# Where two activation buffers lie in SBUF: yT_hi and yT_lo placed second instead of last

## The reference, cut to what matters

```python
x = x + tanh(g_xattn[0]) * cross_attention(layernorm(x), ctx, Wq, Wk, Wv, Wo, bo)
y = layernorm(x)
probs = softmax(mean(y, axis=1) @ gate_w)          # per batch element
top_w, top_i = top_k(probs, 2); top_w = top_w / top_w.sum()
for e in range(8):
    hmid = gelu(y @ w1[e] + b1[e])                 # 256 -> 1024
    out = out + combine[:, e] * (hmid @ w2[e] + b2[e])   # 1024 -> 256
x = x + tanh(g_ffn[0]) * out
```

## Time and profile before

| | |
|---|---|
| median of three runs | 343.83 us (343.82 to 344.36) |
| profiled execution, its own time | 343.83 us |
| its span, first to last instruction | 342.0 us |
| instructions | 5736 |
| TensorE matmul busy | 320.2 us (94%) |
| VectorE, ScalarE, GpSimd busy | 234.5, 166.1, 78.6 us |
| mean granted TensorE clock | 0.986 |

### The profile page before, as it was taken

The page is one execution under the profiler, slowest core; times in us unless marked ns, Lnnn a source line. Parts: engine busy times, 40 slices in busy tenths (PEclk is TensorE's granted clock), DMA queues, the critical chain, the costliest instruction groups (busy, mean ns, idle before and its releaser), DMA issues.

```text
span 342.0 us, 5736 instructions
## 1 busy us (share of the span) xinstructions
PE 320.2 (94%) x1810; PEld 271.9 (80%) x1810; DVE 234.5 (69%) x551; ACT 166.1 (49%) x580; POOL 78.6 (23%) x153
## 2 busy tenths in 40 slices
PE   6988899999999997688998999999999999999994
PEld 6875798889988996586786888888888888888883
DVE  0796879898799988787758747656575564643642
ACT  1627775667775744844535535444454442321320
POOL 1105335575355533346700000000000000000000
PEclk9999999999999999789999999999999999999998
DMA  7990000000000006007000651000000000110001
GB/s 253 398 108 4 0 2 0 3 1 2 1 0 3 2 7 239 2 0 246 2 0 11 237 183 64 0 0 0 0 3 0 0 0 0 61 63 0 33 31 61
DMA packets 19678, 17.26 MB, mean 50 GB/s; under 512 B 10949, under 2 KB 16198, under 8 KB 19526
## 3 DMA queue, kind: packets, MB, share of 16 engines
q1 hardware_dynamic: 19376, 16.43, 15.8%
q10 hardware_dynamic: 278, 0.53, 0.5%
HBM read 14.86 MB, written 2.10 MB: 50 GB/s over the span
## 4 chain that ended last, share of the span: by engine, by line
PE 72%; DVE 12%; ACT 7%; DMA 3%; POOL 3%; issue 2%; SPq 0%; DVEq 0%; ACTq 0%; POOLq 0%
PE ps L945 22%; PE ps L947 22%; PE ps L946 21%; ACT sx L495 5%; DMA wq_sb<-in_L_xattn_Wq_dram 3%; DVE mx L757 2%; PE ps L1046 2%; DVE pT_lo L721 2%; DVE a_lo L670 1%; ACT pT_hi L507 1%; DVE sm L730 1%; PE ps L1012 1%; PE ps L1177 1%; PE ps L1063 1%; PE ps L1120 1%
## 5 line engine op out<-in xcount | busy, mean ns | idle before, releaser
L570 ACT ACTIVATE gel<-ps,b1sel 128x512 f32<-128x512 f32 x64 | 44.1, 689 | 103.7 <-PE ps L947 103.7
L905 DVE CAST h_hi<-gel 128x512 fp32r<-128x512 f32 x64 | 27.8, 434 | 68.5 <-ACT gel L570 68.2
L495 ACT ACTIVATE sx<-ps,mx 128x64 f32<-128x64 f32 x128 | 38.1, 326 | 34.6 <-DVE mx L757 34.6
L945 PE MATMUL ps<-h_hi,w_hi 128*128 128x512 f32 x128 | 50.8, 397 | 0.0
L945 PE MATMUL ps<-yT_hi,w_hi 128*128 128x512 f32 (+1 forms) x128 | 50.2, 392 | 0.0
L947 PE MATMUL ps<-yT_hi,w_lo 128*128 128x512 f32 (+1 forms) x128 | 49.9, 390 | 0.0
L947 PE MATMUL ps<-h_hi,w_lo 128*128 128x512 f32 x128 | 49.9, 390 | 0.0
L946 PE MATMUL ps<-h_lo,w_hi 128*128 128x512 f32 x128 | 49.9, 390 | 0.0
L946 PE MATMUL ps<-yT_lo,w_hi 128*128 128x512 f32 (+1 forms) x128 | 49.9, 389 | 0.0
L907 DVE TENSOR_TENSOR h_lo<-gel,h_hi 128x512 fp32r<-128x512 f32 x64 | 45.2, 706 | 2.2
L945 PE MATMUL ps<-vw,pT_hi 128*128 128x256 f32 x128 | 37.9, 296 | 6.2 <-DVE pT_lo L721 6.2
(11 more groups left out here) (135 smaller groups left out, 608.9 us busy)
## 6 DMA issues: line engine op xcount, KB each, us to landing
stage_w<-in_L_ffn_w_dram SPq DMA_DIRECT2D x8, 1024.0 KB, 6.4
out_dram<-xt SPq DMA_DIRECT2D x8, 256.0 KB, 2.5
xt<-in_x_dram SPq DMA_DIRECT2D x2, 512.0 KB, 9.3
wq_sb<-in_L_xattn_Wq_dram SPq DMA_DIRECT2D x1, 1024.0 KB, 9.0
wv_sb<-in_L_xattn_Wv_dram SPq DMA_DIRECT2D x1, 1024.0 KB, 11.0
wo_sb<-in_L_xattn_Wo_dram SPq DMA_DIRECT2D x1, 1024.0 KB, 14.0
xt<-in_x_dram SPq DMA_DIRECT2D x1, 1024.0 KB, 16.5
wk_sb<-in_L_xattn_Wk_dram ACTq DMA_DIRECT2D x1, 512.0 KB, 4.6
```

Source lines behind the costliest of these rows:

```text
L495: last = nc.scalar.activation(sx[:, par, c0:c0 + M], ps[:, 2 * par + 1, c0 - BANK:c0 - BANK + M], ACT.Exp, bias=mx[:, par, h:h + 1], accum ...
L570: nc.scalar.activation(gel[:, f % 2, :], ps[:, 4 + f % 2, :], ACT.Gelu, bias=b1sel[:, b, slot, f:f + 1]).then_inc(gelu_done, 1)
L905: nc.vector.tensor_copy(h_hi[:, f % 4, :], gel[:, f % 2, :]).then_inc(hhi_ready, 1)
L945: mm(acc, hi_w, hi_x, start=start, stop=False)
```

## The change

The two declarations of `yT_hi` and `yT_lo` move from the end of the area `second` to the common cursor, right behind `xt`. No instruction, wait, semaphore, loop or DMA is edited.

```diff
     xt = place("xt", [P, NT, D])
+    yT_hi = place("yT_hi", [P, KD, NT * P], f32r)
+    yT_lo = place("yT_lo", [P, KD, NT * P], f32r)
     ident = place("ident", [P, P])
...
     xn = place("xn", [P, 2, D], at=second)
-    yT_hi = place("yT_hi", [P, KD, NT * P], f32r, at=second)
-    yT_lo = place("yT_lo", [P, KD, NT * P], f32r, at=second)
     stage_w1.append(place("stage_w1_1", [P, KD, F], at=second2))
```

## The result

The changed kernel is slower. In the first comparison it took 348.59 us (four runs, 347.52 to 349.94) against 344.1 us, ratio 1.0131 with a 95% interval of 1.0094 to 1.0169. Two later comparisons on other occasions gave 1.0114 (1.0076 to 1.0151) and 1.0080 (1.0055 to 1.0105). The runs of the kernel before spread more than the first three had shown, 342.8 to 347.4 us over the later comparisons; so effects under some 1 us are read from the traces, not from the times.

A forecast was written before the change was run, and what follows sets the result against it. It took TensorE's matmul pace to bound the expert phase, while engines wait for one another in attention. All terms were 0: span 342.0 us plus 1.83 us around it gave 343.8 us, range 343.3 to 344.5.

The forecast's parts named there:

- What bounds the kernel: Expert phase, about 154 to 336 us: TensorE never idle, time is number of matmuls times their pace, 0.227 us.
- First, who lies over whom: Overlaying of SBUF tensors: nothing lies over `yT` before or after, other tensors keep their distances; 0 us.
- Second, alignment: Start remainders: only `yT` changes for lines over 64 bytes, and no DMA reads or writes it; 0 us.
- Third, whether speed depends on the place: Engines reading or writing `yT` at its new place: equal shapes at different places showed one pace; taken as 0 us.
- the upper bound: First layer's 384 matmuls at the scores' pace, 0.2329 against 0.227 us: at most 2.3 us more.
- The slower rival: First layer: TensorE reads `yT` at 16 to 48 KB at the scores' pace; 346.1 us, chance 0.05.
- The rule of the Trainium skill: SBUF access: only the port pair shared by VectorE and GpSimd causes contention, place within a partition does not; 0 us.
- The clock's rival: TensorE's clock fall at 141 to 148 us: spared, 342.0 us, chance 0.03; another fall, 346.0 us, chance 0.02.
- Its own spread: Whole kernel, no effect: spread of three runs, within 0.54 us, and one shared instruction; 343.3 to 344.5 us.
- The 0.7 us: Whole kernel: "within 0.2%", about what a measurement can tell from no change; chance 0.87.

The follow-up runs named there:

- high_64_off: Kernel before with 64 spare bytes ahead of `yT_hi`, only the two `yT` buffers moving: 346.87 us, ratio 1.0074.
- low_same_of_256: Changed kernel with 192 spare bytes behind `yT_lo`, so `yT` stays low and every later tensor goes up: 345.51 us, ratio 1.0023.
- all_64_off: Kernel before with 64 spare bytes behind `xt`, so every tensor but `xt` is 64 bytes higher: 344.46 us, ratio 1.0002.
- the probe of the attention groups: Separate kernel of attention's matmul groups behind transposes, weights moved back by d = 0 to 240 bytes: 24 `vw` matmuls 2.953 us at 0, 2.896 at 32.

## Why the prediction was wrong

It said 343.8 us, no change, range 343.3 to 344.5; measured 348.3 to 348.6.

- **What bounds the kernel**: right. The expert phase is matmuls times pace, and as nothing hides TensorE there, all of the pace's loss reached the end.
- **First, who lies over whom, 0 us**: right; high_64_off has the cost and low_same_of_256 is without it, and neither changes which tensors overlie each other.
- **Second, alignment, 0 us from the DMAs**: the step that failed. It worked out that `yT` alone changes its start modulo 128, and then looked only at who else might use that line, the DMAs. It did not ask against which operand a matmul's start counts, though the same line had the numbers for it: `yT` 160,320 bytes down, the weights 32,768 up, 64 modulo 256 apart in their shifts. What the runs showed in its place: with 64 bytes between the two starts the phase is 2.46 us longer (high_64_off), with everything moved by 64 bytes 0.07 us (all_64_off), and with the changed kernel's difference of 192 it is 2.97 us longer.
- **Third, whether speed depends on the place, value 0**: this failed with it. The comparisons in the earlier trace rows were of equal differences. Every placement in them, `h`, `yT`, slots 0 and 1, has the difference 0, since all these tensors are multiples of 256 bytes long and lie in chains from one cursor. Four places with one pace looked like four tests and were one. Also the scores of the earlier trace rows have the difference 0; their seven distances are 235, 233, 236, 224, 231, 236 and 228 ns, and the probe of the attention groups has the very same seven behind two transposes at d = 0, without any change of place. So the upper bound had the right size, 6 ns, by luck, for another reason.
- **The slower rival**, 346.1 us at 0.05: its price, 384 x 5.9 ns = 2.3 us, is what the first layer lost. It left out the second layer, 0.8 us of settling (it expected 0.227 us there), and its cause, low places, was wrong: seven moving places from 32,960 to 209,600 bytes had one pace.
- **The rule of the Trainium skill** ("SBUF — State Buffer", section "Who interferes with whom"): the section names the shared port pair as the only cause of contention and does not speak of places in so many words; that place costs nothing was concluded from its "only". What it says on the port pair agrees with the earlier trace rows; the conclusion fails, since 64 bytes of place cost 2.5 us here. The Trainium skill's page "TensorE: Matmul & The Clock Gate", Part 2, says that loading the next weights does not take read bandwidth from the running matmul. No run here measures bandwidth, but the starts of the two operands matter to the pace, 226.7 to 234.4 ns in steps of 16 bytes, so they are not without effect on each other. That it is the two reads that meet is my reading; the runs show the dependence on the difference and not the mechanism.
- **The clock's rival**: the clock does move from run to run, and more than the earlier trace rows had suggested. In the profiled pair it makes 1.65 of the 4.6 us. Whether the late rise at the start comes more often with this layout is open: three profiles of three have it, against one of eight, but up to 4.4 us, where the clock rises in the kernel before, TensorE's starts are the same in both traces to 1 ns.
- **Its own spread, 0.5 us from three runs**: too narrow; more runs of the same kernel spread over 4.5 us. The 0.7 us that a measurement was said to tell from no change rests on the same three runs.

The account of the profiled pair: 2.3 first layer + 0.8 second layer (together 2.97 by the phase's ends) + 1.05 late rise + 0.6 falls of the clock = 4.6 us, which is the difference of the spans, 346.67 - 342.04.

## What to carry to other kernels

A change of placement is not free by being only a declaration: for 512-column matmuls of 32-bit operands with a weight load each, keep the starts of moving and stationary operand equal modulo 256, by rounding the cursors to 256 bytes and, where tensors of other lengths lie between, each tensor's start; here that is worth 3 us of 344. It is no rule for other shapes: with 256 columns difference 0 was the slowest of the four tried, and 32 bytes apart the products with `vw` took 0.07 us less of 2.75 in the kernel. When a trace is to show that something doesn't matter, ask first whether it varies in the rows compared: four tensors laid out by one rule are one sample. And when a pace is the bound, read start distances to the nanosecond over a long stretch (187 against 183 starts in 42 us), since the mean durations moved by only 5 in 390.

## What the runs showed of the hardware that was not expected

- The pace of back to back 128x512 matmuls depends on the two operands' start difference modulo 256: 226.7 ns at 0 and 240, 228.9 at 64, 230.7 to 234.4 at the other multiples of 16.
- It has a memory: behind a stream with another difference one to eight matmuls pass before the pace is 227 again, behind two transposes mostly nine or more.
- With 256 columns difference 0 is the slowest of four (120.0 against 113.8 ns at 192), with 64 columns all are 112 ns (at 192 the first seven alone, then the clock fell), the transposes 109.2 ns at every difference.
- The clock falls in different places from run to run: in the changed kernel's three profiles twice for 3.4 us (136.2 and 149.8), and once near 31 us in the other two; in the kernel before's one for 6.8 us at 141.1.
